# Cross-attention over 64 batches taken in pairs: the order of TensorE's work, and the buffers and banks that go with it

## The reference, cut to what matters

```python
def _L0_xattn_ref(query, key_value, ...):          # 64 batches, 32 queries, 257 keys, 16 heads of 16
    q = (query @ Wq + bq);  k = (key_value @ Wk + bk);  v = (key_value @ Wv + bv)
    attn = jnp.einsum('bhqd,bhkd->bhqk', q, k) * scale
    attn = jax.nn.softmax(jnp.clip(attn, -CLAMP, CLAMP), axis=-1)
    x = jnp.einsum('bhqk,bhkd->bqhd', attn, v)
    return x @ Wo + bo
x = x + _L0_xattn_ref(_layernorm(x), ctx_768, ...)
x = x + _L0_attn_ref(_layernorm(x), ...)           # a second attention, over the batches
x = x + _L0_ffn_ref(_layernorm(x), ...)            # 8 experts, the best two per token
```

## Time and profile before

| | us |
|---|---|
| median of three runs (613.3 to 617.66) | 616.09 |
| the profiled execution | 618.4 |
| its span, first to last instruction | 616.6 |
| scores of batch 0 start | 18.35 |
| scores of batch 63 start | 332.19 |
| first matmul after the stage (L1231) | 340.68 |

### The profile page before, as it was taken

The page is one execution under the profiler, slowest core; times in us unless marked ns, Lnnn a source line. Parts: engine busy times, 40 slices in busy tenths (PEclk is TensorE's granted clock), DMA queues, the critical chain, the costliest instruction groups (busy, mean ns, idle before and its releaser), DMA issues.

```text
span 616.6 us, 21930 instructions
## 1 busy us (share of the span) xinstructions
PE 587.1 (95%) x8431; PEld 482.4 (78%) x8431; DVE 460.1 (75%) x1072; ACT 348.2 (56%) x768; POOL 329.9 (54%) x481
## 2 busy tenths in 40 slices
PE   8999999999999999999999999998898989899996
PEld 3888878888788887888887788884577777676595
DVE  4688867888577886777777765888676877768494
ACT  3677868777686787778776156454322323223362
POOL 3367858778576787678874311111455565554000
PEclk9999999999999999999999999997999999999999
DMA  8634644867354755875400797258233333342793
GB/s 243 161 82 98 189 158 115 241 183 206 94 188 125 228 157 177 197 233 156 145 17 3 301 413 281 68 172 278 85 116 123 114 124 127 104 131 95 274 342 84
DMA packets 65398, 102.13 MB, mean 166 GB/s; under 512 B 15280, under 2 KB 41968, under 8 KB 64400
## 3 DMA queue, kind: packets, MB, share of 16 engines
q1 hardware_dynamic: 59440, 84.59, 43.6%
q0 software_dynamic: 4992, 15.34, 7.5%
q10 hardware_dynamic: 864, 0.79, 0.5%
HBM read 69.43 MB, written 31.27 MB: 163 GB/s over the span
## 4 chain that ended last, share of the span: by engine, by line
PE 60%; POOL 15%; issue 11%; DVE 9%; DMA 2%; ACT 1%; DVEq 0%; POOLq 0%; SPq 0%; ACTq 0%
PE bank L1960 12%; PE bank L1047 7%; PE bank L1054 7%; PE bank L1079 6%; PE scores L1960 5%; PE scores L1095 4%; PE scores L1068 4%; PE bank L1989 4%; POOL hA L721 3%; POOL lA L717 3%; POOL hA L713 2%; POOL Mb L754 1%; POOL tm L745 1%; POOL whl L784 1%; PE scores L1231 1%
## 5 line engine op out<-in xcount | busy, mean ns | idle before, releaser
L853 DVE TENSOR_SCALAR Pm<-scores 128x514 f32<-128x514 f32 x128 | 88.1, 688 | 55.5 <-PE scores L1068 54.3
L969 ACT ACTIVATE Pm<-Pm,nm 128x257 f32<-128x257 f32 x256 | 115.8, 505 | 2.5 <-DVE nm L858 2.5
L858 DVE TENSOR_REDUCE nm<-Pm 128x2 f32<-128x514 f32 x128 | 87.5, 683 | 2.2
L964 ACT ACTIVATE PT<-bank 128x512 f32<-128x512 f32 x64 | 38.2, 597 | 76.7 <-PE bank L1079 76.7
L1047 PE MATMUL bank<-hA,wH 128*128 128x258 f32 x256 | 75.2, 304 | 1.0 <-issue 1.0
L1960 PE MATMUL bank<-W,xh 128*128 x208 | 66.8, 402 | 6.1 <-DVE xl L1855 5.7
L1079 PE MATMUL bank<-cst,Pm 128*128 128x128 f32 x512 | 70.0, 279 | 0.0
L1047 PE MATMUL bank<-hA,wL 128*128 128x258 f32 x256 | 69.3, 281 | 0.2 <-issue 0.2
L1054 PE MATMUL bank<-wH,hA 128*128 128x256 f32 x256 | 69.1, 281 | 0.0
L1054 PE MATMUL bank<-wL,hA 128*128 128x256 f32 x256 | 68.9, 280 | 0.0
L1905 ACT ACTIVATE sg<-sg 128x512 f32<-128x512 f32 x39 | 24.7, 632 | 74.8 <-DVE sg L1803 69.1
(11 more groups left out here) (289 smaller groups left out, 1464.2 us busy)
## 6 DMA issues: line engine op xcount, KB each, us to landing
w_d<-whl SPq DMA_DIRECT2D x64, 256.0 KB, 3.1
W<-w_d SPq DMA_DIRECT2D x6, 2048.0 KB, 16.7
wst<-in_W1T SPq DMA_DIRECT2D x32, 256.0 KB, 3.7
cg<-g_d SPq DMA_DIRECT2D x16, 512.0 KB, 5.4
cx<-in_ctxT SPq DMA_DIRECT2D x31, 258.0 KB, 3.0
cx<-in_ctxT SPq DMA_DIRECT2D x62, 129.0 KB, 3.5
bb<-in_b SPq DMA_DIRECT2D x8, 512.0 KB, 6.6
W<-w_d SPq DMA_DIRECT2D x5, 512.0 KB, 5.0
```

Source lines behind the costliest of these rows:

```text
L853: v.tensor_scalar(Pm[:, i % 2, 2 * p:2 * p + 2, :], S4[:, 2 * p:2 * p + 2, 0:NK], -CLAMP, CLAMP, ALU.max, ALU.min).then_inc(s_cl, 1)
L858: v.tensor_reduce(nm[:, i % 2, 2 * p:2 * p + 2], Pm[:, i % 2, 2 * p:2 * p + 2, :], AX.X, ALU.max, negate=True).then_inc(s_nm, 1)
L964: a.activation(PT[:, i % 2, 0, :, :].rearrange("p a b -> p (a b)"), held("p", i, 0)[:, :], ACT.Copy).then_inc(s_pte[0], 1)
L969: a.activation(Pm[:, i % 2, g, :], Pm[:, i % 2, g, :], ACT.Exp, bias=nm[:, i % 2, g:g + 1]).then_inc(s_ex, 1)
```

## The change

The four loops go over pairs k of batches A = 2k, B = 2k+1. On TensorE body k is: scores A; weighted sums of both batches of pair k-2; scores B; eight transpositions for each of the two batches of pair k-1; K and V of both batches of pair k+1. Within `scores` the wait for the clips of the batch before is now made per half: groups 0 and 1 wait for its first clip, groups 2 and 3 for the second. The weighted sums leave `S4`: both batches of a pair share one of banks 4 to 7, a new user "o" in `uses`, given back by `total` of both. `Pm`, `tm`, `Os`, `rc`, `nm` get four buffers for two, `Vs` six for four, since results now live a pair longer. 

The order of the other engines follows: VectorE clips A twice in a row, then sums two batches; ScalarE's last two exponentials of B come at the head of the next body, with the side work behind them (`others`), ahead of the copies of the transposed weights; GpSimd normalises two batches at once and does the four splits of a pair in one body. In `pace` one wait is for one batch earlier, as batch i's transpositions now stand later.

```diff
-        Pm = put("Pm", [128, 2, 4, NK])
         kT = put("kT", [128, 2, 2, NKP])
         QF = put("QF", [128, 2, 2, 2 * NQ])
-        Vs = put("Vs", [128, 4, 2, 8, 2, VH])
+        Vs = put("Vs", [128, 6, 2, 8, 2, VH])
...
-        tm = put("tm", [128, 2, 4, VH])
-        Os = put("Os", [128, 2, 4, VH])
+        tm = put("tm", [128, 4, 4, VH])
+        Os = put("Os", [128, 4, 4, VH])
         Mb = put("Mb", [128, 2, 4, 16])
-        rc = put("rc", [128, 2, 4])
-        nm = put("nm", [128, 2, 4])
+        rc = put("rc", [128, 4, 4])
+        nm = put("nm", [128, 4, 4])
...
+        Pm = put("Pm", [128, 4, 4, NK])
...
-        pO = S4[:, 3, 272:272 + 4 * VH]
...
-        for i in range(-1, T + 1):
-            if 1 <= i:
-                uses += [(("p", i - 1, p), s_pte[p], i) for p in range(2)]
-            if i + 1 < T:
-                uses += [(("k", i + 1, p), s_ke, 2 * (i + 1) + p + 1) for p in range(2)]
-            if i + 1 < T:
-                uses += [(("v", i + 1), s_ve, i + 2)]
+        for k in range(-1, NPAIR + 2):
+            if 2 <= k:
+                uses += [(("o", k - 2), s_oa, 2 * (k - 1))]
+            if 1 <= k <= NPAIR:
+                uses += [(("p", i, p), s_pte[p], i + 1) for i in (2 * k - 2, 2 * k - 1) for p in range(2)]
+            if k + 1 < NPAIR:
+                for i in (2 * k + 2, 2 * k + 3):
+                    uses += [(("k", i, p), s_ke, 2 * i + p + 1) for p in range(2)]
+                    uses += [(("v", i), s_ve, i + 1)]
...
         spot = {u[0]: n for n, u in enumerate(uses)}
...
                     if n % 4 == 1:
-                        sp.wait_ge(s_t, 2 * i)
+                        sp.wait_ge(s_t, 2 * (i - 1))
...
-                    if i >= 2:
-                        g.wait_ge(s_oa, i - 1)
-                    g.tensor_tensor(tm[:, i % 2, :, :], Vt[:, i, :, :],
-                                    Pm[:, i % 2, :, NK - 1].unsqueeze(2).broadcast_to([128, 4, VH]), ALU.mult
+                    if i >= 4:
+                        g.wait_ge(s_oa, i - 3)
...
...
                 spread(0)
-                g.wait_ge(s_qb, 1)
+                spread(1)
+                g.wait_ge(s_qb, 2)
                 split(1, 3)
-                for i in range(T + 2):
-                    if i + 1 < T:
-                        spread(i + 1)
-                    if 1 <= i <= T:
-                        tailpart(i - 1)
-                    j, n = (i + 3) // 2 if i % 2 else (i + 2) // 2, 0 if i % 2 else 2
-                    go = 2 <= j < NPAIR
-                    if go:
-                        split(j, n)
-                    if i >= 2:
-                        norm(i - 2)
-                    if go:
-                        if n == 2:
-                            g.wait_ge(s_m, i - 1)
-                        split(j, n + 1)
+                def others(i):
...
+                for k in range(NPAIR + 3):
+                    A, B2 = 2 * k, 2 * k + 1
+                    j = k + 2
+                    if k >= 3:
+                        norm(A - 6)
+                        norm(B2 - 6)
+                        g.wait_ge(s_m, B2 - 5)
+                    if k + 1 < NPAIR:
+                        spread(A + 2)
+                    if j < NPAIR:
+                        split(j, 0)
+                    if k + 1 < NPAIR:
+                        spread(B2 + 2)
+                    if 1 <= k <= NPAIR:
+                        tailpart(A - 2)
+                        tailpart(B2 - 2)
+                    if j < NPAIR:
+                        split(j, 1)
+                        split(j, 2)
+                        split(j, 3)
+                    if k + 1 < NPAIR + 2:
+                        others(A)
+                        others(B2)
...
                 def clip(i, p):
                     v.wait_ge(s_s, 2 * i + p + 1)
-                    if i >= 2:
-                        v.wait_ge(s_t, 2 * (i - 2) + p + 1)
-                        v.wait_ge(s_tm, i - 1)
-                    if i >= 2 and p:
-                        v.wait_ge(s_o, i - 1)
-                    v.tensor_scalar(Pm[:, i % 2, 2 * p:2 * p + 2, :], S4[:, 2 * p:2 * p + 2, 0:NK], -CLAMP, CLAMP,
+                    if i >= 4:
+                        v.wait_ge(s_t, 2 * (i - 4) + p + 1)
+                        v.wait_ge(s_tm, i - 3)
+                    v.tensor_scalar(Pm[:, i % 4, 2 * p:2 * p + 2, :], S4[:, 2 * p:2 * p + 2, 0:NK], -CLAMP, CLAMP,
                                     ALU.max, ALU.min).then_inc(s_cl, 1)
...
                 def total(i):
-                    v.wait_ge(s_o, i + 1)
+                    v.wait_ge(s_o, 2 * (i // 2) + 2)
                     v.wait_ge(s_tm, i + 1)
-                    if i >= 2:
-                        v.wait_ge(s_m, i - 1)
-                    v.tensor_tensor(Os[:, i % 2, :, :].rearrange("p a b -> p (a b)"), pO[:, 0:4 * VH],
-                                    tm[:, i % 2, :, :].rearrange("p a b -> p (a b)"), ALU.add).then_inc(s_oa, 1)
+                    if i >= 4:
+                        v.wait_ge(s_m, i - 3)
+                    o = 4 * VH * (i % 2)
+                    v.tensor_tensor(Os[:, i % 4, :, :].rearrange("p a b -> p (a b)"), held("o", i // 2)[:, o:o + 4 * VH],
+                                    tm[:, i % 4, :, :].rearrange("p a b -> p (a b)"), ALU.add).then_inc(s_oa, 1)
...
-                for i in range(T + 3):
-                    if i < T:
-                        clip(i, 0)
-                        negmax(i, 0)
-                        clip(i, 1)
-                        if i >= 1:
-                            ptevac(i - 1)
-                        negmax(i, 1)
-                    if 2 <= i < T + 2:
-                        total(i - 2)
-                        if i == T:
-                            ptevac(i - 1)
-                        recip(i - 2)
-                    if i >= 3:
-                        otevac(i - 3)
+                def others(i):
...
+                for k in range(NPAIR + 3):
+                    A, B2 = 2 * k, 2 * k + 1
+                    if k < NPAIR:
+                        clip(A, 0)
+                        clip(A, 1)
+                    if 2 <= k < NPAIR + 2:
+                        total(A - 4)
+                        total(B2 - 4)
+                    if k < NPAIR:
+                        negmax(A, 0)
+                        clip(B2, 0)
+                        if k >= 1:
+                            ptevac(A - 2)
+                        negmax(A, 1)
+                        if k >= 1:
+                            ptevac(B2 - 2)
+                        clip(B2, 1)
+                        negmax(B2, 0)
+                        negmax(B2, 1)
+                    if k == NPAIR:
+                        ptevac(A - 2)
+                        ptevac(B2 - 2)
+                    if 2 <= k < NPAIR + 2:
+                        recip(A - 4)
+                        recip(B2 - 4)
+                    if k >= 3:
+                        otevac(A - 6)
+                        otevac(B2 - 6)
+                    if k < NPAIR:
+                        others(A)
+                        others(B2)
...
-                    if i >= 4:
-                        a.wait_ge(s_o, i - 3)
-                    a.activation(Vs[:, i % 4, :, :, :, 0:16].rearrange("p c g s e -> p (c g) s e"),
+                    if i >= 6:
+                        a.wait_ge(s_o, i - 5)
+                    a.activation(Vs[:, i % 6, :, :, :, 0:16].rearrange("p c g s e -> p (c g) s e"),
                                  held("v", i)[:, :].rearrange("p (g s e) -> p g s e", g=16, s=2), ACT.Copy
...
-                for i in range(-1, T + 1):
-                    if 1 <= i:
-                        ptevac(i - 1)
-                    if 0 <= i < T:
-                        exps(i, 0)
-                        exps(i, 1)
-                    if i + 1 < T:
-                        kevac(i + 1, 0)
-                        kevac(i + 1, 1)
-                    if 0 <= i < T:
-                        exps(i, 2)
-                        exps(i, 3)
-                    if i + 1 < T:
-                        vevac(i + 1)
+                def others(i):
...
+                for k in range(-1, NPAIR + 1):
+                    A, B2 = 2 * k, 2 * k + 1
+                    if k >= 1:
+                        exps(B2 - 2, 2)
+                        exps(B2 - 2, 3)
+                        others(A)
+                        others(B2)
+                        ptevac(A - 2)
+                    if 0 <= k < NPAIR:
+                        exps(A, 0)
+                        exps(A, 1)
+                    if k >= 1:
+                        ptevac(B2 - 2)
+                    if 0 <= k < NPAIR:
+                        exps(A, 2)
+                        exps(A, 3)
+                    if k + 1 < NPAIR:
+                        kevac(A + 2, 0)
+                        kevac(A + 2, 1)
+                        vevac(A + 2)
+                    if 0 <= k < NPAIR:
```

(62 more changed lines are left out.)

38 lines of the change are left out of this document (19 added, 19 removed).

## The result

| | before | after |
|---|---|---|
| median of four runs, us | 615.48 (613.3 to 617.66) | 641.65 (639.64 to 644.7) |
| the profiled execution | 618.4 | 642.67 |
| its span | 616.6 | 640.6 |
| its mean granted clock | 0.994 | 0.985 |
| scores of batch 0, of batch 4, of batch 62 | 18.35, 35.81, 327.49 | 20.83, 38.63, 351.94 |

The changed kernel is slower: 1.042 times the time before, with a 95% interval of 1.038 to 1.046. The forecast was 612.7, "same". The places in time say where the loss lies: 2.8 us until batch 4, 21.6 us in the 29 bodies between batch 4 and batch 62 (313.31 against 291.68), 0.9 us at the end. What follows the stage takes what it took (274.6 against 275.9).

The account below looks back on a forecast made before the run. TensorE's own sequence was taken to set the pace, the other engines having slack. Bodies -6.4, filling +2.5 and end +0.5 sum to -3.4 us, from a median of 616.09 to 612.7 us; range 606 to 619.

Parts of the forecast that it names:

- pauses marked 'issue' ... I leave both as they are: Stretch between scores of batches 4 and 62: query projections and issue pauses, like one of 1.42 us, stay unchanged.
- 29 bodies, their phases: Steady state, batch 4 to batch 62: each two-batch body takes 9.18 us against 9.40, saving 6.4 us in all.
- filling, until batch 4: Start of the stage: two batches' projections precede the first scores; scores of batch 4 at 38.3 against 35.81, 2.5 us lost.
- end, after batch 62: From scores of batch 62 to the next stage: 13.7 us against 13.2, 0.5 us lost.
- rival 1: TensorE's change from weighted sums to scores costs 0.33 us, as scores to weighted sums; 618.8 us, chance 0.14.
- the charge for A's second clip: Second half of scores B waits for A's second clip on VectorE; charged 0.08 us a body.
- rival 3: Everything in favour: no pause from weighted sums to scores, no clip wait, cheaper transpositions; 605.5 to 609 us, chance 0.15.
- rival 4: Each change of tile shape on TensorE costs the same full emptying, four changes instead of six; 602.3 us, chance 0.07.
- Other engines: VectorE, ScalarE and GpSimd, worked on by present durations, stay off TensorE's path, the nearest with 0.3 to 0.4 us to spare.
- Rival 2: VectorE, or ScalarE behind side work at its head, runs late and delays TensorE; 627 us if 0.5 us late, chance 0.08.
- rival 6: Context load comes too late for the splits, slack falling from about 14 us to 7 at most; counted into Rival 2.
- Rival 5: Clock falls in the first two bodies, where TensorE stands about 1.5 us; given no chance.

## Why the prediction was wrong

The step that failed is "pauses marked 'issue' ... I leave both as they are". Its own test was "if 'issue' pauses ... move by more than 3 us", and they moved by 12.5; the bodies, which were to be shorter than 9.4 us, were so undisturbed (9.34) but 10.8 on average. The prediction took from the earlier trace rows that such a pause happens, and didn't ask what made it, where it stands, or what the change does to that place. What the runs show in its place: TensorE stands until a packet of its own instructions has come, and joining the weighted sums of two batches into one run makes that happen for 15.9 us instead of 3.4. A clock at half speed behind some pauses (up to 4.6 us) and TensorE's wait for ScalarE's copy (4.1 us), both put at nothing, come on top.

The sum, step by step, against the profiled execution of the kernel after:

| term | predicted | found |
|---|---|---|
| 29 bodies, their phases | -6.4 | -1.7 (29 x 0.06) |
| pauses marked issue | 0 | +12.5 (15.9 - 3.4) |
| clock | 0 | up to +4.6 |
| TensorE waiting for ScalarE's copy | 0 | +4.1 |
| filling, until batch 4 | +2.5 | +2.8 |
| end, after batch 62 | +0.5 | +0.9 |
| sum | -3.4 | +23.2 |

The stage grew by 366.02 - 340.68 = 25.3 us and what follows it fell by 1.3, so 2.1 us of the stage are not in the table (0.9 of them TensorE's wait for a clip). The right column is read from one execution and the clock's term is a bound, so it is the order of the terms that can be leant on, not their last digits.

- **Body.** Scores to weighted sums was right, 0.62. Weighted sums to scores was set at 1.22 and is 1.26 (214.28 - 213.02). The pause between the two, which no row had shown, isn't the reason. A single row of the sums takes 0.18 us, so the last of the 128 starts 1.33 - 0.18 = 1.15 us after the first and the pause is 0.11, and weighted sums to transpositions read the same way in the earlier trace rows is 0.67 - (0.74 - 0.18) = 0.11 too. The assumed price was right and rival 1's 0.33 wrong; the 0.04 come from the run itself, where the prediction had put 0.55 twice. Transpositions took 1.72, not 1.68. The largest miss is the charge for A's second clip: 0.08 predicted, 0.17 found (scores B to transpositions 0.79 against 0.62). The signal was right: the second half of the scores started 214.48 - 212.40 = 2.08 us into the body, 0.06 after the clip, where the prediction had 2.07. What was wrong is when that half would have started unhindered. Its first row stands four rows behind the first half's, 0.03 us and not 0.15 (in the first scores of the body the fifth row starts 0.03 after the first). Together 9.34. The run with half the sums has its second half at the same 2.08, so the front of the body is bound by the clips: a cheaper change from weighted sums to scores, as in rival 3, could win nothing, nor could what rival 4 wins ahead of the second scores. What the Trainium skill says under Key Properties of TensorEngine Tiling, that a change of mode drains TensorE, agrees with the trace in that there are pauses at these changes. It disagrees if it is read as an equal price for each, since they are 0.11, 0.11 and, from scores to weighted sums, 0.3.
- **Other engines.** VectorE was judged rightly (1.08 us idle before A's clip, above the 0.5 named). ScalarE was not. Its slack was worked out from durations alone, with the side work at its own length. But its side work waits for a DMA, and in the new order the copy that TensorE needs soonest is queued behind that wait. Rival 2 named "ScalarE behind the side work now at its head", and rival 6 a load that comes too late, but of the context; the load that was late was the expert weights'. The move of the side work shows it: TensorE's wait for the copy goes with it. That it is worth 7.8 us rests on one comparison.
- **Clock.** Rival 5 was given nothing because one pause of 1.42 us had passed without a fall. It didn't fall in the first two bodies, which rival 5 had named; it fell later on, behind one pause of 1.22 us and within one of 3.15, while pauses of up to 2.35 us passed without a fall.
- **Filling and end** were right to 0.4 us each. The scores of batch 1 waited for the clips, as worked out (`0.88 <-DVE Pm L863` at 22.40).

What is shown: longer unbroken runs of short matmuls make the pauses (twice the run in the old order, half the run and two runs apart in the new), and traffic adds to them. That the pauses are TensorE waiting for instructions is read from the queue. In the ten traces of this case there are 95 pauses marked issue of TensorE's matmuls between 30 and 470 us, and every one ends 1.20 to 1.66 us after a q8 packet does. No run changed the fetch itself, and why a fetch comes as late as it does stays open: the one behind the pause that ends at 271.21 started at 268.3, with the DMA engines next to idle. How much of the loss is clock alone is a bound, not a measurement. No version of the pairs came near the old kernel with all work done: the best of them is at 1.03 to 1.04, and even without any pause the 1.7 us of the bodies would not pay the 3.7 at both ends.

## What to carry to other kernels

Before you put two runs of many small matmuls next to each other, look at where "issue" pauses stand today and what is in the instruction queue then; here the orders with transpositions or projections between shorter runs had 1.9 to 3.4 us of pauses, and the joined ones 12.6 to 15.9 with the same traffic. Work a new order out per engine queue with its waits, not with durations alone: an instruction that may wait for a DMA belongs behind whatever the engine that sets the pace needs next. A saving of 0.2 us in a body of 9 is smaller than what any of these can take.

## What the runs showed that I had not expected

- TensorE stood for 0.2 to 3.2 us with all semaphores met, inside the run of weighted sums or soon behind it, each time until 1.20 to 1.66 us after a 16 KB packet of instructions had ended; in the variants a pause reached 4.6 us. Ten of the twelve came back in front of the same matmuls on another chip.
- The granted clock fell to 1.2 GHz for 3.4 us behind a pause of 1.22 us (ends at 194.18) and for 6.8 us from within one of 3.15, although the mean over the execution is still 0.985; a pause of 2.35 us (ends at 271.21) had no such effect.
- From the end of a clip on VectorE to the matmul it releases took 0.06 us where other matmuls were still running (214.42 to 214.48), and 0.15 where TensorE stood (batch 1: the first clip ends at 22.26, the scores start at 22.40).
- 0.6 us of matmul per body could be left out without any gain in an undisturbed body (9.34 both times), while the kernel gained 15.8 us.
